# Sixteen x buffers, fourteen token tiles through the row ring and reordered shared sums in layer 1 of a mixture-of-experts kernel

## The reference

```
x = x + 0.5 * ffn(layernorm(x))
x = x + mamba(layernorm(x))
x = x + 0.5 * ffn(layernorm(x))

def ffn(x):                                   # 16 experts, top 4, hidden size 176
    scores = sigmoid(x @ gate_w.T) + gate_b
    weights, indices = top_k(scores, 4);  weights /= weights.sum(-1)
    shared = (silu(x @ w1s) * (x @ w3s)) @ w2s
    routed = sum over the 4 chosen experts e of  weight_e * (silu((x @ w1[e]) * (x @ w3[e])) @ w2[e])
    return shared + routed
```

## Time and profile before

| | us |
|---|---|
| median of 3 runs | 560.35 |
| lowest and highest | 560.19, 562.23 |
| the profiled execution | 561.91 |
| span of the profiled execution, first to last instruction | 560.1 |

### The profile page before, as it was taken

One profiled execution on the slowest core, in us unless ns is written; L12 is line 12 of the kernel. 1 busy time (PEld: TensorE's weight loads), 2 busy tenths in 40 slices (PEclk: granted clock), 3 DMA queues, 4 the chain that ended last, 5 costly groups with the idle time before them and its releaser, 6 DMA issues.

```text
span 560.1 us, 13322 instructions
## 1 busy us (share of the span) xinstructions
PE 481.5 (86%) x3206; PEld 449.0 (80%) x3207; DVE 436.5 (78%) x1464; ACT 367.2 (66%) x1109; POOL 352.7 (63%) x364
## 2 busy tenths in 40 slices
PE   2969569999999999958996960599999999999865
PEld 2857449999999999947884950389999999999754
DVE  5889857777889888875998579656777888887836
ACT  2687836777777777767874571656777777777610
POOL 3699947546777777766411416276457777777774
PEclk9999678999999999979999885579999999999988
DMA  8992044666665566654100480036445555666666
GB/s 274 393 393 99 30 121 127 180 170 184 176 201 169 167 169 171 179 150 113 57 2 19 134 262 17 21 112 178 138 138 169 169 169 173 169 161 174 178 186 209
DMA packets 61150, 88.27 MB, mean 158 GB/s; under 512 B 9499, under 2 KB 46363, under 8 KB 61107
## 3 DMA queue, kind: packets, MB, share of 16 engines
q0 software_dynamic: 13728, 37.50, 26.3%
q1 hardware_dynamic: 47379, 50.29, 26.2%
HBM read 57.22 MB, written 30.54 MB: 157 GB/s over the span
## 4 chain that ended last, share of the span: by engine, by line
PE 60%; DVE 16%; issue 10%; DMA 5%; POOL 4%; ACT 4%; SPq 0%; POOLq 0%; ACTq 0%; DVEq 0%
PE bank L1414 29%; PE bank L1465 15%; PE bank L1435 6%; POOL mamba_room L616 3%; PE bank L1476 3%; PE bank L1475 3%; DMA ys_scratch<-ring_f 2%; DVE xres L1144 2%; PE bank L1487 1%; DMA raw_shared<-in_w13s 1%; PE bank L1633 1%; DMA ring_f<-xn_scratch,tokidx 1%; PE bank L1551 1%; DVE stage L1039 1%; DVE ring_f L1110 1%
## 5 line engine op out<-in xcount | busy, mean ns | idle before, releaser
L1465 PE MATMUL bank<-w_routed,ring_r 128*128 x790 | 120.8, 283 | 5.0 <-DVE ring_r L990 4.5
L1465 PEld LDWEIGHTS bank<-w_routed,ring_r 128*128 128x128 f32 x790 | 110.4, 189 | 7.4 <-issue 7.4
L578 POOL DMA_INDIRECT ring_f<-xn_scratch,tokidx x80 | 77.2, 965 | 58.3 <-DVE tokidx L1121 22.5
L695 ACT ACTIVATE ring_r<-bank 128x256 fp32r<-128x256 f32 x158 | 60.8, 385 | 68.9 <-PE bank L1476 66.8
L1414 PE MATMUL bank<-w_routed,ring_r 128*128 x480 | 100.6, 346 | 0.0
L578 POOL DMA_INDIRECT ring_g<-xn_scratch,tokidx x78 | 74.5, 955 | 35.4 <-PE bank L1435 20.2
L1414 PE MATMUL bank<-w_routed,ring_x 128*128 x468 | 94.6, 337 | 0.0
L1414 PEld LDWEIGHTS bank<-w_routed,ring_r 128*128 128x128 f32 x480 | 78.8, 196 | 0.1
L1414 PEld LDWEIGHTS bank<-w_routed,ring_x 128*128 128x128 f32 x468 | 74.1, 190 | 0.0
L988 DVE TENSOR_TENSOR ring_r<-bank,ring_r 128x128 fp32r<-128x128 f32 x158 | 45.8, 290 | 30.5 <-ACT ring_r L695 28.6
L547 POOL TENSOR_TENSOR w_routed<-raw_routed,w_routed 128x512 fp32r<-128x512 f32 (+1 forms) x38 | 55.3, 1494 | 19.7 <-ACT w_routed L671 19.6
(11 more groups left out here) (190 smaller groups left out, 1075.5 us busy)
## 6 DMA issues: line engine op xcount, KB each, us to landing
ys_scratch<-ring_f SPq DMA_DIRECT2D x152, 128.0 KB
raw_routed<-in_w13r SPq DMA_DIRECT2D x6, 704.0 KB, 12.2
xn_scratch<-w_routed SPq DMA_DIRECT2D x32, 128.0 KB, 4.0
raw_routed<-in_w2r SPq DMA_DIRECT2D x6, 512.0 KB, 12.7
raw_routed<-in_w13r SPq DMA_DIRECT2D x8, 352.0 KB, 6.4
xres<-in_x_in SPq DMA_DIRECT2D x4, 512.0 KB, 7.3
raw_routed<-in_w2r SPq DMA_DIRECT2D x8, 256.0 KB, 7.2
shared_scratch<-raw_ring SPq DMA_DIRECT2D x16, 128.0 KB, 1.7
```

The lines of the kernel that those rows point to most:

```text
L578: pool.indirect_dma_start(xg[j % XG], None, xn_dram, bass.IndirectOffsetOnAxis(ap=tokidx[:, j:j + 1], axis=0)).then_inc(s_g[j % XG], 16)
L695: act.activation(hT[b][0], p_hT[b][:, 0:2 * P], ACT.Copy).then_inc(s_hhi, 1)
L1465: last = pe.matmul(p_y[b][:, 0:D], a, v, start=(q == 0), stop=(q == 4))
```

## The change

Nothing is changed in layer 0, except that a few constants become pairs (layer 0, layer 1). In layer 1:

- **x buffers.** 16 instead of 8: four more lie in the room of the shared expert's up weights, four in a stage tile that held the first six hidden tiles of the shared expert. `lead` grows from 7 at gather 17 to 15 around gathers 39 to 47, and falls to 4 by gather 73. PE's loop body holds 16 slots instead of 8 and takes the buffer's number from the place in the body.
- **Row ring.** It carries 14 tiles (56 rows) instead of 12. 44 of the rows (instead of 32) are issued among the x gathers, from gather 43 on, 11 for every 9 gathers; DVE adds them from step 29 on, 8 steps for 7 rows. The gate on output sums starts with row 40 and asks for n + 24. The other 12 rows follow the last x gather. Two tiles (8 rows) are left for `combine`.
- **Hidden reads.** SP's six reads ahead of the slot loop move behind its loop of y writes and ahead of the last three writes, after a wait for the last x transpose; they go into the room of x buffers.
- **Sums.** DVE adds sums 0 to 2 after the 56 early rows, sums 3 to 6 after tile 14's rows, then tile 15's rows, then sum 7. The results of tiles 14 and 15 wait for sum 7.
- ACT's and DVE's loops end at step 29's mark instead of step 35's; what follows is unrolled.

The core of the diff:

```diff
-PE_UN = 2 * UN
...
-EARLY_TILES = 12
-EARLY = EARLY_TILES * TOPK
+EARLY_TILES = (12, 14)
+EARLY = [t * TOPK for t in EARLY_TILES]
 ROWS = 6
-XG = 8
+XG = (8, 16)
 YL = 3
-EARLY_FIRST, IN_LOOP = 35, 32
+IN_LOOP = (32, 44)
+ADDED_FROM = 29
 LEADS = ((8, 3), (12, 4), (14, 5), (17, 6), (46, 7), (62, 6), (73, 5), (NS, 4))
-BEHIND_Y, GATED = 34, 28
-LATE = NT - EARLY_TILES
+BEHIND_Y, GATED = (34, 24), (28, 40)
...
-SUMS_AFTER = {12: (0, 1), 13: (2, 3), 14: (4, 5, 6, 7)}
+SUMS_AFTER = {13: (0, 1, 2), 14: (3, 4, 5, 6), 15: (7,)}
...
+        xg += ([raw_shared[:, h, b * D:(b + 1) * D] for h in range(2) for b in range(2)]
+               + [r0(b * D, (b + 1) * D) for b in range(XG[1] - XG[0] - 4)])
...
-        hidb = [r0(b * H, (b + 1) * H) for b in range(HID_AHEAD)]
+        hidb = [ring_f[:, b * H:(b + 1) * H] for b in range(HID_AHEAD - 1)] + [ring_g[:, 2 * D:2 * D + H]]
...
-        def early_after(n):
-
-            return max(4 * (n // TOPK) + EARLY_FIRST, EARLY_FIRST + 7 * n // 5)
-
-        def early_step(n):
-
-            return early_after(n) if n < IN_LOOP else NS + (n - IN_LOOP) * 5 // 8
-
-        def lead(j):
-
-            return next(k for end, k in LEADS if j < end)
+        def x_before(f, k):
+
+            return tiles_of(k, XG[0]) if f and k < XG[0] else 0
+
+        def early_after(f, n):
+
+            return 43 + 9 * n // 11 if f else max(4 * (n // TOPK) + 35, 35 + 7 * n // 5)
+
+        def early_step(f, n):
+
+            if n >= IN_LOOP[f]:
+                return NS + (n - IN_LOOP[f]) * 5 // 8
+            return ADDED_FROM + 8 * n // 7 if f else early_after(f, n)
+
+        def lead(f, j):
+
+            if f == 0 or j < 17:
+                return next(k for end, k in LEADS if j < end)
+            return min(XG[1] - 1, j * 11 // 30 + 1) if j < 44 else min(XG[1] - 1, max(4, XG[1] - (j - 43) * 2 // 5))
 
         def rows_fetched(f, n):
 
-            return f * -(-(EARLY - n % ROWS) // ROWS) + n // ROWS + 1
+            return f * -(-(EARLY[0] - n % ROWS) // ROWS) + n // ROWS + 1
...
-                    sp.wait_ge(s_rt, 2)
-                    for t in range(HID_AHEAD):
-                        hid_in(t)
                 else:
                     sp.wait_ge(s_et, NT)
                     sp.wait_ge(s_rt, 1)
@@ -524,10 +531,14 @@
                 with sp.Fori(1 if f else SHARED_BEHIND[-1] // UN, NS // UN) as i:
                     for k in range(UN):
                         y_out(f, i, k)
+                if f:
+                    sp.wait_ge(s_xt, 2 * STEPS)
+                for t in range(HID_AHEAD if f else 0):
+                    hid_in(t)
                 for k in range(YL):
...
-                if t >= EARLY_TILES:
+                if t >= EARLY_TILES[1]:
...
-                if j > lead(j):
-                    pool.wait_ge(s_xt, f * STEPS + NT + j - lead(j))
-                pool.indirect_dma_start(xg[j % XG], None, xn_dram,
+                if j > lead(f, j):
+                    pool.wait_ge(s_xt, f * STEPS + NT + j - lead(f, j))
+                pool.indirect_dma_start(xg[j % XG[f]], None, xn_dram,
                                         bass.IndirectOffsetOnAxis(ap=tokidx[:, j:j + 1], axis=0)
-                                        ).then_inc(s_g[j % XG], 16)
+                                        ).then_inc(s_g[j % XG[f]], 16)
...
-                if n >= GATED:
-                    pool.wait_ge(s_y, f * NS + min(NS, n + BEHIND_Y))
+                    pool.wait_ge(s_ea, f * EARLY[0] + n - ROWS + 1)
+                if n >= GATED[f]:
+                    pool.wait_ge(s_y, f * NS + min(NS, n + BEHIND_Y[f]))
...
-                    for n in range(EARLY):
-                        if early_after(n) == j:
+                    for n in range(EARLY[f]):
+                        if early_after(f, n) == j:
                             fetch_early(f, n)
-                for n in range(EARLY):
-                    if n >= IN_LOOP:
+                for n in range(EARLY[f]):
+                    if n >= IN_LOOP[f]:
                         fetch_early(f, n)
                 pool.wait_ge(s_y, (f + 1) * NS)
-                for t in range(EARLY_TILES, NT):
+                for t in range(EARLY_TILES[f], NT):
...
-                if 2 * pair >= EARLY_TILES:
-                    dve.wait_ge(s_cd, combined_to(1, min(2 * pair + 1, NT - 2)))
+                if 2 * pair >= EARLY_TILES[1]:
+                    dve.wait_ge(s_cd, combined_to(1, 2 * pair + 1))
                 dve.scalar_tensor_tensor(xp, p_yS[pair % 4][:, :], 0.5, xp, ALU.mult, ALU.add).then_inc(s_sa, 1)
 
             def combine_last(t):
 
-                if t == NT - 1:
-                    dve.wait_ge(s_sa, NT // 2)
                 for q in range(TOPK):
...
+                    for pair in SUMS_AFTER[EARLY_TILES[1] - 1]:
+                        shared_sum(pair)
+                    for t in range(EARLY_TILES[1], NT):
                         combine_last(t)
...
-                    pe.wait_ge(s_g[k], 16 * (f * tiles_of(k, XG) + i * (PE_UN // XG) + c // XG + 1))
-                    pe.wait_ge(s_xlo, base + i * PE_UN + c - 1)
+                    b, k = c % 2, c % XG[f]
+                    pe.wait_ge(s_g[k], 16 * (x_before(f, k) + i + c // XG[f] + 1))
+                    pe.wait_ge(s_xlo, base + i * XG[f] + c - 1)
...
-                pipeline(pe, NS, [(LAG_X, pe_x(f, base)), (LAG_H, pe_hidden(base)), (LAG_Y, pe_out(f)),
-                                  (LAG_E, pe_experts), (LAG_T, pe_ht(f, base))], PE_UN)
+                pipeline(pe, NS, [(LAG_X, pe_x(f, base)), (LAG_H, pe_hidden(f, base)), (LAG_Y, pe_out(f)),
+                                  (LAG_E, pe_experts(f)), (LAG_T, pe_ht(f, base))], XG[f])
```

More of the change, by code:

```diff
@@ L46 @@
 MEASURED = 8
-SCALED = ((0, 8), (8, EARLY_TILES))
+SCALED = ((0, 8), (8, EARLY_TILES[0]))
 TABLE_AFTER = 75
@@ L129, in build @@
         hT = [[ring_r[:, 1024 + (b * 2 + h) * 256:1024 + (b * 2 + h + 1) * 256] for h in range(2)] for b in range(2)]
-        ring_g = sb("ring_g", [P, (XG - UN) * D])
-        xg = [ring_f[:, k * D:(k + 1) * D] for k in range(UN)] + [ring_g[:, k * D:(k + 1) * D] for k in range(XG - UN)]
+        ring_g = sb("ring_g", [P, (XG[0] - UN) * D])
+        xg = [ring_f[:, k * D:(k + 1) * D] for k in range(UN)] + [ring_g[:, k * D:(k + 1) * D] for k in range(XG[0] - UN)]
         hid = [ring_f[:, 1024 + b * 2 * P:1024 + (b + 1) * 2 * P] for b in range(2)]
@@ L134, in build @@
         yb = [ring_f[:, 1536 + b * D:1536 + (b + 1) * D] for b in range(2)]
-        y_last = [xg[k] for k in (XG - 1, UN, UN + 1)]
+        y_last = [xg[k] for k in (XG[0] - 1, UN, UN + 1)]
         ring_h = ring_f[:, :].bitcast(f16)
@@ L272, in build @@
         s_xw = [sem(f"xn_written{k}") for k in range(NG)]
-        s_g = [sem(f"gathered{k}") for k in range(XG)]
+        s_g = [sem(f"gathered{k}") for k in range(XG[1])]
         s_xt = sem("x_transposed")
@@ L613, in combine @@
                     n = t * TOPK + q
-                    beside(f, n - EARLY)
-                    room = (cgl if f else cg)[t - EARLY_TILES]
+                    beside(f, n - EARLY[f])
+                    room = (cgl if f else cg)[t - EARLY_TILES[0]]
                     pool.indirect_dma_start(room[:, q, :], None, ys_dram[0:tiles_before(t) * P, :],
@@ L1130, in stage @@
                 def stage(i, c):
-                    for n in range(EARLY):
-                        if early_step(n) == c + LAG_T + 1:
+                    for n in range(EARLY[f]):
+                        if early_step(f, n) == c + LAG_T + 1:
                             row_added(f, n)
@@ L1185, in add @@
                 n = t * TOPK + q
-                rows = (cgl if f else cg)[t - EARLY_TILES]
+                rows = (cgl if f else cg)[t - EARLY_TILES[0]]
                 dve.scalar_tensor_tensor(xres[:, t, :], rows[:, q, :], wk[:, n:n + 1], xres[:, t, :],
@@ L1417, in _, with pe_experts, stage @@
             e_reg = [[pe.alloc_register(f"expert{g}_{k}") for k in range(UN)] for g in range(2)]
-            def pe_experts(i, c):
-                if c % UN == 0:
-                    pe.reg_load(e_reg[c // UN % 2], te[0:1, ds(i * PE_UN + c, UN)])
+            def pe_experts(f):
+                def stage(i, c):
+                    if c % UN == 0:
+                        pe.reg_load(e_reg[c // UN % 2], te[0:1, ds(i * XG[f] + c, UN)])
+                return stage
             def routed_weights(c):
```

50 lines of the change are left out of this document (24 added, 26 removed).

## The result

The changed kernel takes **556.81 us** (median of 20 runs, 552.59 to 560.59) against 560.61 us for the kernel before (20 runs, 558.75 to 563.96). The ratio is **0.9923, with a 95% interval of 0.9899 to 0.9946**: faster by 0.8%. Timed once more beside the first experiments it was 557.86 us and 0.9956 (0.9931 to 0.9981). The forecast was 554.4 us, with a range of 551.6 to 557.8, and 556.6 us for rival 1, in which the clock falls: the first median lies inside the range, the second 0.06 us above it.

What follows compares the result with a forecast made beforehand. Matmul engine bounds the slot loop, then GpSimd's late row gathers the end; with loop end 2.3 and loads 0.5 us later, sum 7 at 551.55 + 0.4 + 2.15 = 554.1, off the median 554.4 us; range 551.6 to 557.8.

Steps and rivals of the forecast that it cites:

- rival 1: Granted clock falls between slot loop and pairs, costing 2.2 us: 556.6 us; chance 0.15.
- Gather 43: GpSimd in layer 1: with lead 15 it starts at 416.25, eight gathers further on, worth 10.1 us.
- Row 51: Last row added ahead of the last slot's hT: issued at 526.6, landing at 529.4, with VectorE waiting for it.
- the last gather: GpSimd's last row gather: issued at 541.8, with its gates about 542.5, landing at 545.3.
- The loop's end: Last output matmuls of layer 1's slot loop end at 531.5 instead of 529.18, 2.3 us later.
- The hidden loads: SP's six loads moved behind the y writes: 0.3 us gained at the loop's head, first pair's loads 0.5 us late.
- held write: A y write held up ahead of the moved hidden loads can add 0 to 1 us; 0.3 taken.
- Pairs, sums, end: Pairs run through at 2.20 us, pair 7 ends at 550.4; sum 6, four additions, sum 7 at 551.55.
- Rival 2: Rows land in 4.7 instead of 2.8 us, loads and a held write cost in full: 557.7 us; chance 0.14.
- A GpSimd at the old time: A gate holds GpSimd so its last gathers come at the old time: 560.3 us; chance 0.05.
- a slower loop body: The matmul engine's 16-slot body waits for code at three jumps back: 562.8 to 568.5 us; chance 0.04.
- rival 3: Rows in time, GpSimd at its bare pitch, the slot loop's end not moved: 551.6 us; chance 0.10.

Runs made afterwards that it cites:

- with 13: The changed kernel with leads of at most 13 instead of 15, all else as changed: 563.42 us, 1.0031 to the kernel before.
- second profile: The changed kernel timed and profiled once more, unaltered: 557.86 us, 0.9956 to the kernel before; its profiled execution took 553.78 us.
- early loads: The changed kernel with the six hidden loads issued one by one behind the y writes of slots 66 to 71: 553.61 us, 0.9869 to the kernel before.

## Why the prediction was right, and where it was not

**GpSimd: right, to a microsecond.** Gather 43 was forecast at 416.25, that is 414.83 with the earlier start, and came at 414.10. The 0.7 us between are about the 0.8 that the loop gained at its head when the hidden loads left it. Row 51 was to follow 110.3 us later and did after 109.9; the last gather, 540.4 to 541.1 with the shift, came at 540.41. That this had to be bought with rows, and that the lead of 15 is needed, the runs with buffers alone and with 13 show on GpSimd's timeline.

**The loop's end: later, but by less than forecast, and the mechanism half.** Forecast were 2.3 us later for row 51, less 0.3 at the start. Measured from the layer's first gather, the end moved by 1.47 and 1.05 us; without the rows and with the hidden loads moved it is at 168.01, so the denser rows cost 1.8 to 2.2 us and the loads' move gave some 0.8 instead of 0.3. But VectorE doesn't wait for row 51, as the forecast has it: the row is added at 527.11 with no wait ahead. The last slots' additions stand in a full VectorE between one hT and the next; moved behind the loop they give back 1.1 to 1.5 us. For row 51 landing was not the limit, the order of VectorE's work was.

**The hidden loads: the term that was mis-sized.** Forecast 0.5 us, bounds 0 to 1.2; measured 1.9 and 1.2 ahead of pair 0 in the two profiles, and in the second 0.77 more for pair 3, whose loads the forecast had in time. The step looked at the two loads of pair 0 alone. The matmul engine turns pair 1 before it multiplies pair 0, so four loads at half a microsecond each stand ahead of the first product, and loads here land 3.2 us after issue (the median of the seven into that ring; the forecast's ends were 2.7 and 3.5). It said that each part was issued in time and overlooked which instruction needs how many.

**The clock: rival 1 came in one of the two profiles, and its chance was too small.** It had 0.15; of the six traces with late loads and an unfilled pause three show the fall. The argument against it was that layer 1's end kept its clock through pauses; but the pauses there were short (0.24 and 0.30 us), and the loads, costed too low, made this one 1.6. The Trainium skill (TensorE: Matmul & The Clock Gate, Part 1) has the half rate as the default that activity lifts; the run with fourteen transposes in the pause agrees, at 1.00 from 528 to 548 with the loads just as late.

**The number: in part luck.** Rival 1's time, 556.6 us, is close to both medians, but not by its price of 2.2 us alone. In the first profile, from the layer's first gather, the last output ends 0.8 us earlier than forecast (2.3 us later with the held write, 1.47 measured) and the loads cost 1.4 us more, so that pair 0 starts 0.6 us late; the fall costs 1.6, since pair 1 starts 3.86 us after pair 0, where it was 2.28 before. The forecast's own case is there too: in the second profile, with the clock held, it is 194.1 us from the first gather to the end, and 193.7 were forecast. There the loop's end, forecast 1.2 us too late, covers most of the 1.5 us that the loads cost beyond their 0.5.

**Pairs, sums, end: right.** The pairs follow each other at 2.17 us (2.20 forecast) from pair 1 on in the first profile, and the last sum stands behind four additions of 2.04 us. That pair 4's wait ran only beside the bound was right too: taken away alone it is worth 0.1%, not to be told from nothing. No pair waits for a sum, but one of the two profiles has pair 3 wait for its loads.

**Rivals 2 to 5.** Of rival 2 the loads in full came, and more (1.9 and 2.0 us in all); that row 51 lands late did not, since VectorE adds it without a wait. A GpSimd at the old time and a slower loop body are not there; the longer body alone is at 0.9987. A loop's end that doesn't move (rival 3) isn't there either.

## What to carry to other kernels

When a load is moved from a stretch that it disturbs to one close to its use, count how many loads the consumer's first *product* needs, in the order in which that engine works, and issue them as soon as the last reader of their room is done, between other work of the queue. Buffers that let an engine run ahead move its last work only if the work behind them can move up too (here 0.8 us with the buffers alone, 11.5 with the rows); look for the gate that the saved time falls into. At the tail, put each sum of several kinds where its last operand arrives, so that one addition and one result are left when the last operand comes.

## What was not expected of the hardware

A pause of 1.6 us on the matmul engine, after which the granted clock is 0.50 for about 3 us, in one execution of the changed kernel, and waits of 0.29 and 0.93 us with the clock at 1.00 throughout in another: the same kernel on the same inputs loses the clock at this place in one execution and keeps it in the next, for 1.4 us between the loop's end and pair 7's. Work without any use in the pause (14 transposes, 1.69 us) left the clock at 1.00 in the one execution that was traced. And the mean clock of a whole execution doesn't tell whether it fell here: 0.920 with early loads and no fall, 0.921 in the first profile of the changed kernel, with one.
